# Seventh expert's second linear and scatter in parts of 2, 2 and 1 tiles; eighth expert's bias as a product of ones

## What is computed

```python
idx = jnp.argmax(probs, axis=-1)                 # each token goes to one of 8 experts
buf = jnp.zeros((E, C, D)).at[idx, pos_safe].set(x, mode='drop')   # C = 640 rows an expert
hmid = jax.nn.relu(jnp.einsum('ecd,edf->ecf', buf, w1) + b1[:, None, :])
ybuf = jnp.einsum('ecf,efd->ecd', hmid, w2) + b2[:, None, :]
y_tok = ybuf[idx, pos_g] * (prb * kept)[:, None]
y = jnp.nan_to_num(y, nan=0.0, posinf=10000.0, neginf=-10000.0)
x = x + y
x = x + adj @ (layernorm(x) * W)                 # the third layer, 8 blocks of 512 columns
```

## Time and profile before

| | before |
|---|---|
| median of 3 runs | 1015.59 us |
| the runs | 1015.41, 1015.59, 1019.68 us |
| the profiled execution | 1016.05 us, span 1013.7 us |
| mean granted TensorE clock | 0.993 |
| busy: PE, PEld | 993.1 us (98%), 529.6 us (52%) |
| busy: DVE, ACT, POOL | 416.6 us (41%), 310.8 us (31%), 179.0 us (18%) |

### The profile page before, as it was taken

The page is one execution under the profiler, slowest core; times in us unless marked ns, Lnnn a source line. Parts: engine busy times, 40 slices in busy tenths (PEclk is TensorE's granted clock), DMA queues, the critical chain, the costliest instruction groups (busy, mean ns, idle before and its releaser), DMA issues.

```text
span 1013.7 us, 12482 instructions
## 1 busy us (share of the span) xinstructions
PE 993.1 (98%) x3618; PEld 529.6 (52%) x3618; DVE 416.6 (41%) x1443; ACT 310.8 (31%) x601; POOL 179.0 (18%) x216
## 2 busy tenths in 40 slices
PE   8999999999999999999997999989999999999997
PEld 4555555555555444444443588734545445454554
DVE  6323223323313344334434156562453424535266
ACT  4644645645541000000001254241312223122231
POOL 4110010010010122121222144551011010110101
PEclk9999999999999999999999899989999999999999
DMA  9995675366104788888854743167464564645300
GB/s 363 421 416 196 258 319 241 133 290 277 56 0 167 296 331 301 309 306 305 323 207 170 266 120 112 31 215 280 166 258 178 188 239 166 257 179 187 156 1 22
DMA packets 41664, 220.57 MB, mean 218 GB/s; under 512 B 6644, under 2 KB 22712, under 8 KB 29430
## 3 DMA queue, kind: packets, MB, share of 16 engines
q1 hardware_dynamic: 38454, 215.21, 55.2%
q0 software_dynamic: 2864, 4.39, 1.3%
q10 hardware_dynamic: 272, 0.13, 0.0%
HBM read 210.29 MB, written 11.62 MB: 219 GB/s over the span
## 4 chain that ended last, share of the span: by engine, by line
PE 93%; ACT 3%; DVE 1%; issue 1%; DMA 1%; DVEq 0%; POOL 0%; SPq 0%; ACTq 0%; POOLq 0%
PE PA L1822 22%; PE PA L1573 22%; PE PA L1593 22%; PE O L1768 3%; PE O L1886 3%; ACT U L682 3%; PE O L1642 3%; PE PA L1551 2%; PE T L1906 2%; PE T L1895 1%; PE SR L1886 1%; PE SM L1886 1%; PE O L1614 1%; PE O L1604 1%; PE O L1863 1%
## 5 line engine op out<-in xcount | busy, mean ns | idle before, releaser
L1822 PE MATMUL PA<-ring,S 128*128 128x512 f32 x512 | 236.0, 602 | 3.4 <-issue 3.4
L1593 PE MATMUL PA<-ring,S 128*128 128x512 f32 x512 | 229.8, 595 | 1.2 <-DMA ring<-in_adj_cols 1.2
L1573 PE MATMUL PA<-ring,U 128*128 128x512 f32 x512 | 226.7, 595 | 0.0
L1573 PEld LDWEIGHTS PA<-ring,U 128*128 128x128 f32 x512 | 94.8, 190 | 106.6 <-issue 106.5
L1593 PEld LDWEIGHTS PA<-ring,S 128*128 128x128 f32 x512 | 95.4, 190 | 102.4 <-issue 98.7
L1822 PEld LDWEIGHTS PA<-ring,S 128*128 128x128 f32 x512 | 92.9, 192 | 103.8 <-issue 100.5
L602 ACT ACTIVATE work<-ring 128x2048 int8<-128x2048 f32 x64 | 122.2, 1910 | 9.0 <-issue 4.7
L1429 DVE TENSOR_TENSOR U<-ring,work 128x512 f32<-128x512 f32 x112 | 81.8, 735 | 89.4 <-PE SR L1886 45.5
L750 ACT ACTIVATE work<-T,work 128x64 f32<-128x64 f32 x112 | 29.0, 310 | 66.8 <-PE T L1895 54.2
L847 POOL DMA_INDIRECT disp_d<-work x32 | 31.9, 997 | 96.4 <-DVE work L1263 89.1
L859 POOL DMA_INDIRECT y_d<-R,work x40 | 39.3, 983 | 51.1 <-DVE R L1331 41.1
(11 more groups left out here) (271 smaller groups left out, 1086.4 us busy)
## 6 DMA issues: line engine op xcount, KB each, us to landing
ring<-in_adj_cols SPq DMA_DIRECT2D x52, 2048.0 KB, 9.3
ring<-in_adjT_cols SPq DMA_DIRECT2D x32, 2048.0 KB, 7.2
ring<-in_adj_cols SPq DMA_DIRECT2D x8, 1024.0 KB, 13.6
work<-in_w SPq DMA_DIRECT2D x16, 256.0 KB, 2.8
ring<-in_Wr SPq DMA_DIRECT2D x1, 4096.0 KB, 12.1
ring<-in_Wr SPq DMA_DIRECT2D x2, 2048.0 KB, 13.3
disp_d<-U SPq DMA_DIRECT2D x4, 650.0 KB, 19.4
work<-disp_d SPq DMA_DIRECT2D x8, 325.0 KB, 3.7
```

Source lines behind the costliest of these rows:

```text
L1573: mm = nc.tensor.matmul(out_T[:, :], X[:, t * D:(t + 1) * D], ring[slot][t // HT][:, (t % HT) * BW:(t % HT + 1) * BW], start=n == 0, stop= ...
L1593: mm = nc.tensor.matmul(PA[k % 2][:, :], S[:, t * D:(t + 1) * D], ring[slot][t // HT][:, (t % HT) * BW:(t % HT + 1) * BW], start=t == 0, s ...
L1822: mm = nc.tensor.matmul(PA[slot][:, :], S[:, t * D:(t + 1) * D], ring[1][t // HT][:, (t % HT) * BW:(t % HT + 1) * BW], start=t == 0, stop= ...
```

## The change

`parts_of` gives `LPARTS` for the seventh expert too, so its second linear on TensorE, its work on VectorE and its scatters on POOL run in parts of 2, 2 and 1 tiles. The third part's products go to the bank T[0], and TensorE first waits until ACT has copied the eighth expert's transposes out of it. VectorE gives `s_ye` with the third part's read, which comes after the second part is finished. The counts of `s_yp` and `s_y` go by `done_parts`.

For the eighth expert, each tile's second linear starts with a product of one row of ones (as weights) and one row of the bias; the four products then add to it. VectorE no longer reads and adds the bias: `scale` multiplies straight from PSUM into `e_y`, followed by `finite`.

```diff
--- before.py
+++ after.py
@@ -270,7 +270,10 @@
         YB = [O[0], O[1], T[0]]
 
         def parts_of(e):
-            return EPARTS if e < E1 - 1 else LPARTS
+            return EPARTS if e < E1 - 2 else LPARTS
+
+        def done_parts(e):
+            return 2 * e + max(0, e - (E1 - 2))
 
 
 
@@ -853,7 +856,7 @@
             for i in range(E1 // 2):
                 for par in range(2):
                     for n, (lo, hi) in enumerate(parts_of(2 * i + par)):
-                        pool.wait_ge(s_y, i * 4 + par * 2 + n + 1)
+                        pool.wait_ge(s_y, done_parts(2 * i + par) + n + 1)
                         alone(pool)
                         for q in range(lo, hi):
                             nc.gpsimd.indirect_dma_start(y_d, bass.IndirectOffsetOnAxis(ap=e_idx[par][:, q:q + 1], axis=0),
@@ -1308,7 +1311,7 @@
                 def read(n):
 
                     lo, hi = parts_of(e)[n]
-                    dve.wait_ge(s_yp, e * 2 + n + 1)
+                    dve.wait_ge(s_yp, done_parts(e) + n + 1)
                     alone(dve)
                     return nc.vector.tensor_tensor(tiles(e_y[par][:, lo * D:hi * D], hi - lo), tiles(YB[n][:, 0:(hi - lo) * D], hi - lo),
                                                    e_b2[par].unsqueeze(1).to_broadcast([P, hi - lo, D]), ALU.add)
@@ -1331,7 +1334,7 @@
                     nc.vector.copy_predicated(y, odd, sub).then_inc(s_y, 1)
                     dve.drain()
 
-                dve.wait_ge(s_yp, e * 2 + 1)
+                dve.wait_ge(s_yp, done_parts(e) + 1)
                 alone(dve)
                 if rnd is not None:
                     dve.wait_ge(s_sc2[par], rnd * (16 * CT))
@@ -1339,14 +1342,13 @@
 
                 nc.vector.tensor_copy(e_idx[par], e_tags[par][:, :, 1])
                 if e == E1 - 2:
-                    read(0)
-                    dve.drain()
-                    scale(0)
-                    finite(0)
-                    read(1).then_inc(s_ye, 1)
-                    dve.drain()
-                    scale(1)
-                    finite(1)
+                    for n in range(len(LPARTS)):
+                        some = read(n)
+                        if n == len(LPARTS) - 1:
+                            some.then_inc(s_ye, 1)
+                        dve.drain()
+                        scale(n)
+                        finite(n)
                 elif e < E1 - 1:
                     read(0)
                     dve.drain()
@@ -1356,10 +1358,13 @@
                     scale(1)
                     finite(1)
                 else:
-                    for n in range(len(LPARTS)):
-                        read(n)
+                    for n, (lo, hi) in enumerate(LPARTS):
+                        dve.wait_ge(s_yp, done_parts(e) + n + 1)
+                        alone(dve)
+                        for q in range(lo, hi):
+                            nc.vector.tensor_scalar(e_y[par][:, q * D:(q + 1) * D], YB[n][:, (q - lo) * D:(q - lo + 1) * D],
+                                                    e_tags[par][:, q, 0:1], None, ALU.mult)
                         dve.drain()
-                        scale(n)
                         finite(n)
 
             for e in range(2):
@@ -1761,7 +1766,9 @@
                     turn_rows(1 - par, rnd + par)
                 pe.wait_ge(s_hm, e * (2 * FK) + 2 * FK + 4)
                 pe.wait_ge(s_ye, e + 1)
-                for bank, (lo, hi) in zip(O, EPARTS):
+                for n, (bank, (lo, hi)) in enumerate(zip(YB, parts_of(e))):
+                    if n == 2:
+                        pe.wait_ge(s_xT, e + 2)
                     for q in range(lo, hi):
                         c = q - lo
                         for f in range(FK):
@@ -1786,9 +1793,10 @@
                         pe.wait_ge(s_ye, e + 1)
                     for q in range(lo, hi):
                         c = q - lo
+                        nc.tensor.matmul(YB[n][:, c * D:(c + 1) * D], ones[0:1, :], e_b2[par][0:1, :], start=True, stop=False)
                         for f in range(FK):
                             mm = nc.tensor.matmul(YB[n][:, c * D:(c + 1) * D], e_hm[:, f * CAP + q * P:f * CAP + (q + 1) * P],
-                                                  e_w2[par][:, f * D:(f + 1) * D], start=f == 0, stop=f == FK - 1)
+                                                  e_w2[par][:, f * D:(f + 1) * D], start=False, stop=f == FK - 1)
                     mm.then_inc(s_yp, 1)
 
                 first(0)
```

## The result

The changed kernel takes 1019.02 us in the median of 20 runs (1017.15 to 1022.45), the kernel before 1015.88 us in 20 runs beside them (1015.17 to 1019.71). The ratio is 1.0025, 95% interval 1.0016 to 1.0035, so 1.6 to 3.6 us longer. That is within the 0.5% that I called no change, but outside my range of 1014.3 to 1017.6: I had 0.3 us more, it is about 3. The profiled execution took 1021.41 us with a span of 1019.3, 5.6 us more than the span of before.

The account below looks back on a forecast made before the run. POOL's scatter queue was taken as the bound: its head 1.77 us earlier is spent waiting for the eighth expert, delayed by stall (0.41) and bias products; last scatter 0.2 to 0.3 us later, 1015.9 us, range 1014.3 to 1017.6.

Parts of the forecast that it names:

- What bounds the kernel: POOL's scatter queue for the last two experts sets stage 3's start; an earlier head gains at most 0.35 us.
- the head start: Rival at the eighth expert: added products and stall cost nothing, last scatter 1.1 us earlier, 1014.5 us; 18 in 100.
- the stall: TensorE before the eighth expert's second linear waits for the seventh's last read, now third; costs 0.41 us.
- The bias as a product: Eighth expert's second linear: two more records a tile at 0.111 us each, 0.45 us for each two-tile part.
- a dearer product: Rival in the eighth's second linear: 0.05 us more a record, 0.2 us a part; 22 in 100 with the clock stretch.
- The scale from PSUM: VectorE's scale for the eighth expert: 0.10 us more for two tiles, 0.05 for one, bounds 0 and 0.13.
- The clock stretch: Rival: TensorE's half-clock stretch at stage 3 moves and shows, 1016.3 to 1017.7 us; 22 in 100 with a dearer product.
- The collisions: Rival: PSUM scales leave POOL's scatters alone, no slips in the tail, 1015.6 to 1015.8 us; within the forecast's 60 in 100.
- the slower cases: The clock stretch at stage 3, or a dearer product in the eighth's second linear; together 22 in 100.
- the sum: Eighth expert's path to POOL's last scatter: 655.25 instead of 655.04, 0.2 us later, 0.3 with half the slips.

Follow-up runs that it names:

- the split wait: Changed kernel, but the eighth expert's first two parts wait only for the seventh's first two reads; against the kernel before, ratio 1.0017, on a late chip 1.0059.
- the product of full height: Changed kernel with the bias as a 128-row product (identity times bias), run with the split wait; against the kernel before, ratio 1.0005.
- the full rows: Changed kernel with the bias as a 128-row product, original single wait kept; against the kernel before on late chips, ratios 1.0039 and 1.0032.

## Why the prediction was wrong

**What bounds the kernel**: right. POOL's queue of scatters sets the start of stage 3, and with the head 1.72 us earlier (641.37 measured, 641.32 forecast) nothing is gained, because the eighth expert's first part has 0.35 us of slack. With the split wait and the bias on VectorE, which has the head start and neither the dear product nor the stall, D is 19.53 against 19.60.

**The stall**: right in its mechanism, 0.41 us forecast, 0.47 and 0.50 seen as TensorE's idle time, 0.52 by the split wait. The seventh's last read starts at 647.00 less 3.31 = 643.69 (643.43 forecast). Of these 0.26 us, 0.20 are VectorE's L1330, which took 0.48 us beside POOL's first scatter (at 645.30) and 0.28 in the part before; I had left such collisions out.

**The bias as a product**: this is the step that failed. It stands in the prediction as "I take 0.111 as the step, between 0 [...] and 0.16". Measured is 0.61 us a tile, or 0.31 a record, nearly twice my upper bound. Four tiles ahead of POOL's last wait make 4 x 0.39 = 1.56 us. The sixth scatter came 0.92 us later than forecast (653.94 - 3.31 = 650.63 against 649.71), two tiles' 0.78 and 0.1 of the stall; the last 1.62 us (656.87 against 655.25), four tiles' 1.56. Nothing above 0.1 us is left in that part of the sum. The rival "a dearer product" had a price of 0.05 us a record, a quarter of the true excess of 0.20. Yet the true price would only have moved 1015.9 to about 1017.5, just inside my range; the rest of the way to 1019.02 is told at the end of this section.

Where it is dear can be read at the weight loads. TensorE's weight loads in the timeline, first of the change, then of the product of full height with the split wait:

```profile
651.30 0.29 PEld L1796 LDWEIGHTS O<-work,ones 1*128 1x128 f32 x2
651.72 0.97 PEld L1798 LDWEIGHTS O<-work,U 128*128 128x128 f32 x8
```

```profile
643.14 0.97 PEld L1800 LDWEIGHTS O<-work,U 128*128 128x128 f32 x8
...
649.93 0.19 PEld L1556 LDWEIGHTS PA<-ring,ident 128*128 128x128 f32 x1 [0.24 <-issue]
```

The loads behind the ones product start at 651.72, together with their own product (651.72), and those of the ones product at 651.30, together with theirs (651.31). With full height they start 0.11 us ahead (643.14 and 643.25), that is beside the product before. The one-row loads don't take longer themselves (0.29 us for two, as full ones 0.30). The Trainium skill (TensorE: Matmul & The Clock Gate, "LDWEIGHTS (loading the stationary operand)") says that a load's time goes by columns and not by rows; the trace agrees, 0.29 and 0.30, and yet the rule would have misled, because the price is not in how long a load takes. The Trainium skill (TensorE: Matmul & The Clock Gate, "The mechanism") also says that TensorE pulls a load ahead of products in flight if the load targets a row group that doesn't conflict, or the background buffer. The missing lead fits a load that isn't pulled ahead. The 0.39 us fall on two passages: the ones product steps by 0.41 us instead of 0.22, and the eight records behind it by 1.09 instead of 0.89. That is 0.19 and 0.20 us, and a single load of 128 columns takes 0.19 (649.93). So one load that isn't hidden at each passage would make the price. That is argued from these rows and not shown: no run here varies the rows between 1 and 128, and why TensorE doesn't hide the load stays open.

The price was in the trace of before, and I read the wrong number of it. I took the mean durations, 426 and 379 ns. The starts in the timeline of before say more:

```profile
34.65 0.59 PE L1540 MATMUL SR<-R 128*128 128x256 f32 x2
35.17 0.69 PE L1541 MATMUL SR<-R 2*128 2x256 f32 x2
35.80 1.13 PE L1543 MATMUL O<-R 128*128 128x256 f32 x4
```

From 34.65 to 35.17 and on to 35.80 is 0.52 and 0.63 us; two full products of this width step by 0.43 to 0.44 (644.19 to 644.62 in the timeline after). So one passage into two rows and back costs 0.09 + 0.20 = 0.29 us beyond the records, where the change measured 0.39. With 0.29 a tile my sum would have ended at 655.25 + 4 x 0.29 = 656.4, 1.4 us above the kernel before instead of 0.2.

**The scale from PSUM**: right at its upper bound. A pair takes 0.61 us (650.89), 0.13 above the 0.48 from SBUF. The Trainium skill's rule (VectorE: DVE Perf Modes, "Why PSUM operands drop a tier"), which I had weighed, came out at that size.

**The rivals.** The head start didn't survive. The clock stretch on a chip on time went the harmless way (it didn't fall in the change; where it fell on such a chip, as in the split wait with the product of full height, the stretch behind stage 3's first product was no longer for it, 351.27 us). The collisions: POOL had no slip behind the sixth scatter, but its waits would have hidden one. I had given the slower cases together 22 in 100.

**What the sum didn't hold.** 2.3 of the 3.1 us in the medians are accounted for by D (1.83), the way to stage 3 (0.13) and the rest (0.33); the last two were not in my sum. The rest goes with the kernel's code: 351.0 us behind the first product of stage 3 in the kernel before on either kind of chip, 351.3 in the change (where the clock was up again by then) and with the full rows, 0.30 of it POOL's pause, 351.2 to 351.3 with the bias product alone, without that pause, and 351.6 to 351.7 in the five executions with parts and the bias on VectorE, where VectorE's last addition starts 0.35 us later once more. What ties these pauses to code that is edited elsewhere is open. The lowest runs, 1017.15 and 1015.17, are 1.98 apart. The other 0.8 us I put down to late starts, which no trace but the two shows: 7 of 20 runs of the change are above 1020.6, 3 of 20 of before above 1019.1. That a start comes late, with the low clock behind it, is seen without the ones product too, the four other executions of the change and its split wait don't have it, and so few runs can't tell whether the change makes it more frequent. Nor had I thought that the answer depends on the chip: where signals are late the loss is 5 to 8.5 us by the ratios.

## What to carry to other kernels

Price an instruction of a new shape from start to start across the change of shape, in the timeline, not from the mean duration of its group: here the cost lay between the records' starts, and their durations hid it. A small product between large ones isn't small: one row cost 0.61 us a tile where 128 rows cost 0.22, so fill the height. And an earlier head of a queue is worth only the slack of the next thing that the queue waits for; work that out before paying for it.

## What the runs showed of the hardware

- An fp32 product of 1 row and 128 columns, followed by one of 128 rows, steps by 0.41 us for its two records and delays the whole tile from 1.11 us (full height) to 1.50, in all seven traces that have it at the upper clock. In the two traces that have it at the lower clock the tile takes 2.73.
- On three of five chips the semaphores of TensorE's products come up to 2.2 us later than on the others, from the second expert on (3.4 to 4.7 us with the seventh expert in parts), while the starts of the records keep their 0.111 us. Signals of successive products then come 0.04 us apart, where on time they come 0.43 to 0.54 apart, so they look held and released together. The kernel before takes 6 to 10 us longer there. What holds them is open.
- The granted clock fell in or right behind a TensorE idle time of 3.7 to 3.9 us. In six executions it was back 3 to 7 us later, in two only after 20 to 24 us in which TensorE worked without a gap, both with one-row products. By the mean clocks that happened in 12 of 20 runs with one-row products behind such idle time and in none of 45 without them.
- In two of 20 executions stage 1's first product started late (9.89 and 8.94 us, in the others 8.07 to 8.91), behind 2.71 and 1.91 us of idle time, and the granted clock was 0.50 from 10 to 12 us; the first rows were turned at 36.55 and 35.60 instead of 33.35. In the others the idle time was 1.75 us or less and the clock stayed at 1.00.
- The same operation of POOL, in code that no edit touched, starts 0.48 us behind the one before it in all 13 executions with three parts for the seventh expert, and 0.18 in the seven with two.
